# A four-layer transformer kernel on one core: the row normalization of both attention stages divided over two head pairs, one step to a block of units

## The reference, cut to what matters

```python
def reference(...):
    x = L0_attn_x                                   # (4, 1024, 128)
    x = _layernorm(x + _L0_attn_ref(x, ...))        # 16 heads of 64, causal        (stage s0)
    x = _layernorm(x + _L0_ffn_ref(x, ...))         # gated attention, 8 heads      (stage s1)
    x = _layernorm(x + _L1_attn_ref(x, ...))        # 16 heads of 64, relative bias (stage s2)
    x = _layernorm(x + _L1_ffn_ref(x, ...))         # 16 experts, top 32 tokens
    return x

def _layernorm(x, axis=-1, eps=1e-05):
    m = jnp.mean(x, axis=axis, keepdims=True)
    v = jnp.var(x, axis=axis, keepdims=True)
    return (x - m) / jnp.sqrt(v + eps)
```

## Time and profile before

| | |
|---|---|
| median of 3 runs | 4331.12 us (4328.69 to 4333.49) |
| the profiled execution | 4329.32 us, span of its trace 4327.6 us |
| PE busy | 3832.9 us, 89% of the span |
| DVE busy | 3238.8 us, 75% |
| POOL busy | 2941.0 us, 68% |
| ACT busy | 1926.0 us, 45% |
| mean granted clock of PE | 0.954 of full |
| stage s0 | about 50 to 1150 us |
| stage s2 | about 2550 to 4190 us |

### The profile page before, as it was taken

One profiled execution on the slowest core, in us unless ns is written; L12 is line 12 of the kernel. 1 busy time (PEld: TensorE's weight loads), 2 busy tenths in 40 slices (PEclk: granted clock), 3 DMA queues, 4 the chain that ended last, 5 costly groups with the idle time before them and its releaser, 6 DMA issues. The chain is left out here.

```text
span 4327.6 us, 62571 instructions
## 1 busy us (share of the span) xinstructions
PE 3832.9 (89%) x22170; PEld 2166.8 (50%) x22170; DVE 3238.8 (75%) x5670; ACT 1926.0 (45%) x3478; POOL 2941.0 (68%) x2166
## 2 busy tenths in 40 slices
PE   7998998989788989889899848999999999999964
PEld 4554555545355555555555424555455445545533
DVE  5887868868487877877877647887888788878826
ACT  3443544434354555454455313444444344434423
POOL 2776767757445877877887926777777677767740
PEclk9999999999888999999999958999999999999987
DMA  3000000000110000100100031211222121212121
GB/s 55 23 20 15 24 14 25 10 6 1 40 46 19 28 28 19 38 28 19 33 28 10 6 63 28 43 30 30 40 38 37 30 40 30 45 26 39 19 59 30
DMA packets 98072, 125.87 MB, mean 29 GB/s; under 512 B 28929, under 2 KB 76481, under 8 KB 97761
## 3 DMA queue, kind: packets, MB, share of 16 engines
q1 hardware_dynamic: 97760, 121.86, 13.1%
HBM read 103.69 MB, written 18.12 MB: 28 GB/s over the span
## 5 line engine op out<-in xcount | busy, mean ns | idle before, releaser
L857 POOL TENSOR_TENSOR s_psum_p<-s_psum_p,s_prob 128x1024 f32<-128x1024 f32 (+3 forms) x640 | 1335.5, 2087 | 371.0 <-ACT s_prob L562 320.7
L562 ACT ACTIVATE s_prob<-s_sT 128x1024 f32<-128x1024 f32 (+2 forms) x896 | 791.8, 931 | 843.4 <-DVE s_sT L713 473.8
L459 PE MATMUL s_pv<-s_prob,s_vp 128*64 128x512 f32 (+3 forms) x3584 | 795.7, 565 | 4.8 <-POOL s_prob L842 4.8
L669 DVE CUSTOM_DVE_ANT_0 s_mx<-s_mx,s_strip 128x512 f32<-128x512 f32 x628 | 421.8, 713 | 162.4 <-PE s_mx L415 159.1
L1746 POOL TENSOR_TENSOR s_psum_p<-s_psum_p,s_prob 128x1024 f32<-128x1024 f32 x192 | 462.5, 2409 | 105.9 <-ACT s_prob L1469 104.1
L1469 ACT ACTIVATE s_prob<-s_sT 128x1024 f32<-128x1024 f32 x256 | 262.7, 1026 | 585.5 <-PE s_sT L1333 585.5
L415 PE MATMUL s_mx<-s_bh,s_ah 64*128 64x512 f32 (+2 forms) x1756 | 396.2, 447 | 102.9 <-DVE s_bm L659 58.7
L718 DVE RECIPROCAL s_recip<-s_recip 128x128 f32<-128x128 f32 x512 | 452.5, 921 | 35.5 <-ACT s_recip L509 35.5
L857 POOL TENSOR_TENSOR s_psum_p<-s_prob 128x1024 f32<-128x1024 f32 (+1 forms) x128 | 288.5, 2254 | 197.0 <-ACT s_prob L562 194.3
L459 PEld LDWEIGHTS s_pv<-s_prob,s_vp 128*64 128x64 f32 x3584 | 218.8, 137 | 371.7 <-issue 288.3
L415 PEld LDWEIGHTS s_mx<-s_bh,s_ah 64*128 64x128 f32 x1756 | 165.8, 185 | 449.9 <-issue 191.0
(11 more groups left out here) (291 smaller groups left out, 7256.3 us busy)
## 6 DMA issues: line engine op xcount, KB each, us to landing
s_strip<-bias_rows SPq DMA_DIRECT2D x256, 144.0 KB, 5.7
s_wr<-gated_weights SPq DMA_DIRECT2D x32, 960.0 KB, 4.8
s_near<-bias_rows SPq DMA_DIRECT2D x256, 48.0 KB, 2.0
x<-s_x SPq DMA_DIRECT2D x10, 512.0 KB, 3.4
s_x<-x SPq DMA_DIRECT2D x8, 512.0 KB, 5.1
gated_weights<-s_side_hi SPq DMA_DIRECT2D x8, 480.0 KB, 2.6
gated_weights<-s_side_lo SPq DMA_DIRECT2D x8, 480.0 KB, 2.9
s_x<-in_L_attn_x_dram SPq DMA_DIRECT2D x4, 512.0 KB, 5.3
```

Source lines behind the costliest of these rows:

```text
L459: last = mm(pv[heads(hd), lo:CH], vp[:, g // VP % 2, j, at:at + DH], prob[:, k % PR, hd, lo:CH], start=j == 0, stop=end)
L562: nc.scalar.activation(prob[:, k % PR, :, lo:CH], sT[:, k % 2, :, lo:CH], ACT.Exp, scale=st.scale).then_inc(exp_done, 1)
L669: last = nc.vector.tensor_tensor_reduce(out=mx[:, hd, :], in0=mx[:, hd, :], in1=strip[:, g % 2, hd, first:first + CH], scale=1.0, scalar=N ...
L857: nc.gpsimd.tensor_tensor(out[:, :, lo:CH], src, p[:, :, lo:CH], ALU.add)\
```

## The change

In `Pairs.jobs` the seven steps no longer all stand in pair 1 of the next batch. Steps 0 to 3 stay there, steps 4 to 6 go to pair 2, and each gets a block to itself.

```diff
@@ -165,9 +165,12 @@
         if g > 0:
             out[3].append(("norm", 2 * g - 2))
             out[7 if self.causal or after else 9].append(("norm", 2 * g - 1))
-        if p == 1 and b > 0:
-            for n, u in enumerate((3, 4, 5, 6, 7, 8, 10) if self.causal else (5, 6, 7, 8, 9, 10, 12)):
-                out[u].append(("ln", b - 1, n))
+        if b > 0:
+            first = (3, 5, 7, 9) if self.causal else (5, 7, 9, 13)
+            rest = (3, 5, 9) if self.causal else (5, 7, 11)
+            for n, (of, u) in enumerate([(1, u) for u in first] + [(2, u) for u in rest]):
+                if p == of:
+                    out[u].append(("ln", b - 1, n))
         return out
```

## The result

| | before | after |
|---|---|---|
| median | 4330.07 us (6 runs) | 4380.04 us (4373.02 to 4384.75, 6 runs) |
| ratio to before, 95% interval | | 1.0117 [1.0103, 1.0131] |
| span of the profiled execution | 4327.6 us | 4380.0 us |
| mean granted clock | 0.954 | 0.95 |

What follows compares the result with a forecast made beforehand. PE was taken to set the pace, with DVE close behind and tied to it. Stall 47.5 plus clock 7.5 minus spreading gains 10 and 4 made +41 us on 4329.3, forecast 4372 us, range 4345 to 4392.

Steps and rivals of the forecast that it cites:

- the likeliest case: Whole kernel: stalls of 44 to 52 us in s2 with the smaller clock loss, 4372 us, chance 0.66.
- Part 3, the stall: s2, block 12 of pair 2: DVE's first maximum waits for strips queued behind the late store, 47.5 us lost.
- Part 3's place: s2, first maximum of block 12 in pair 2: the strip wait is on the path, each microsecond also lost by PE.
- The first rival: Block 12 of pair 2: no strip wait, only the gains remain, -14 us, 4317 us, chance 0.07.
- The second: Block 12 of pair 2: PE's other work rides out 6 us of each stall, clock stays up, 4347 us, chance 0.12.
- The third: Behind each stall: PE stays at half clock for 14 us, losing 7 us a time, 4386 us, chance 0.15.
- Part 4, the clock: Behind each of three stalls in s2: some 5 us of PE work at half rate, 7.5 us lost in all.
- a loss of half of that: Behind each stall: half of some 5 us of half-rate PE work is lost, 2.5 us, three times.
- Part 1, spreading in s2: s2: giving each step its own block wins 3.4 us a batch, 10 us in all, bounds 0 and 19.8.
- Step 5 is an 8-column instruction: nothing: s2, pair 2: the sixth of the seven steps, counted from 0, costs no time in its new block.
- Part 2, spreading in s0: s0: at most one step in each block of a pair gives a small gain of 4 us, bounds 0 and 18.
- I take 1.3 us a batch of the 6.0: s0: of the 6.0 us the seven steps cost per batch, spreading wins 1.3 us, 4 us in all.

Runs made afterwards that it cites:

- the repeat: The changed kernel itself, unaltered, run again beside a kernel with filler products on PE: 4384.92 us, ratio 1.0127.
- the narrow additions: Changed kernel with SP's store behind the strips, and POOL's additions cut to 16 of 512 columns in pair 2 of s2: 4324.54 us, ratio 0.9982.
- s0 alone: The changed kernel with the new places of the seven steps only in s0, s2 keeping the old ones: 4338.44 us, ratio 1.0011.

## Why the prediction was right, and which terms were not

The verdict, the range and the mechanism that decides held: the likeliest case came, and 4380 is 8 us above the forecast. Two of the four terms had the wrong sign all the same, so the small distance is in part luck. By its own parts:

- **Part 3, the stall: right.** Waits of 15.4, 15.4 and 11.9 us were in the sum (3.45 + 0.42 + 11.5, and 0.4 + 11.5); the profile has 15.80, 15.88 and 12.82. On the path it is 42.3 us, with what the lower clock behind the stalls costs in it: pairs 2 and 3 take 340.6 us together in the change and 298.3 with the store behind the strips. I had 47.5, since I added 1.6 us each for step 6 in front of it, and in the run with the store behind that cost is there without any stall.
- **Part 3's place: right.** Wherever step 6 stood directly ahead of that maximum and the store ahead of the strips, the stall was there. SP waited 39.5, 36.3 and 37.9 us, where some 30 had been given. The first rival (no stall, 4317) has nothing for it. The second (6 us of each stall ridden out) neither: PE stood 18.2, 18.0 and 15.0 us. The third (the clock costs more, 4386) comes near in its time, above all to the 4384.92 us of the repeat, but not by its reason: the lower clock behind a stall lasted 3.5 to 3.8 us and not 14.
- **Part 4, the clock: right in kind, wrong in size.** The lower clock came behind each stall, for 3.5 to 3.8 us and not 5, but DVE covers it: at most about 2 us against 7.5. The step that failed is "a loss of half of that". It took PE for the engine that sets the pace in block 12, while part 3 had just said that PE waits for DVE there. By the rule of the Trainium skill (TensorE: Matmul & The Clock Gate, Terms), throttled time times one minus the ratio, these 11 us of work at the lower clock would cost an estimated 5.5 us. The measurement differs and decides here: PE's own work does get longer, but not the kernel by as much.
- **Part 1, spreading in s2: wrong sign.** Forecast 10 us won. With the stall away, pair 1 wins 2.5 us a batch (the 3.24 us of PE behind steps 1 and 2 shrank to 1.95, as forecast), but pairs 2 and 3 lose 17.7 us in all (298.3 against 280.6): together some 10 us lost. The steps that failed are "Step 5 is an 8-column instruction: nothing" (1.93 us, and PE stood 1.95) and the length of step 6, 1.90 us taken, 2.86 measured. Both are waits for POOL's additions, as the narrow additions showed. The odd 1.97 us of step 1 was in the rows, and the prediction itself names a wait for POOL as its reason; I weighed it only for a chance to win. It should have been asked of each step: does it meet POOL at work?
- **Part 2, spreading in s0: wrong sign.** Forecast 4 us won, measured 3.6 us lost in the profile of the change and 5.7 between the medians with s0 alone. Steps 2 and 3 alone took 2.20 and 1.95 us there where 1.23 and 1.16 had been, again across POOL's work, while step 6 won 0.4 to 1.1 us. The step that failed is "I take 1.3 us a batch of the 6.0": it took the lengths of the steps as fixed. A longer s0 was among the signs of being wrong, and it came. That these waits are the whole loss of s0 is argued and not shown: no run took POOL's additions away in s0. One reading is that two steps in one block wait for POOL once, and two steps in two blocks can wait twice.
- **The sum.** Forecast 47.5 + 7.5 - 10 - 4 = 41. The runs give 42 for stall and clock together, 10 for the spreading in s2 and 4 to 6 for s0, 56 to 58 us; the medians say 50, and 54.5 in the repeat. The parts were measured in separate runs, each uncertain by a few microseconds, so they do not close to better than that. Stall and clock had been taken 13 us too high, the two terms of spreading 28 to 30 us too low. These errors cancel out in part, and only in part: the total is a better forecast than its terms.

## What to carry to other kernels

Before moving a step, list who waits for its semaphore and what stands in that queue behind the wait. Here a store that nobody was waiting for held up the strip that DVE's very next instruction needed, and the price was the whole latency of store, load and strip pieces, some 15 us each time. Put what is needed soon ahead of what waits for something late; it cost nothing in the kernel before (4332.72 against 4332.76 us) and leaves 5.7 us of the change's loss.

Spreading work evenly over blocks is a gain only if each piece fits beside what the other engines do at that moment. Read a small instruction with a long duration as a wait, and find what ends with it.

## What the runs showed of the hardware that was not expected

- A DVE instruction on 8 columns takes 0.11 us when POOL's additions are short and 1.93 us when it begins during a 128x1024 addition, and ends within 0.05 us of that addition. A 128x1024 multiply of two SBUF operands takes 1.16 to 2.86 us by the same cause. Reductions of one operand are not touched (1.16 to 1.22 us).
- POOL pays as well. In the run with the store behind the strips, its two additions took 5.70 us where step 3 ran beside them, and 4.9 us elsewhere; POOL's timeline, then DVE's:

```profile
3886.47 5.70 POOL L860 TENSOR_TENSOR s_psum_p<-s_psum_p,s_prob 128x1024 f32<-128x1024 f32 x2 [1.96 <-ACT s_prob L565]
```

```profile
3888.43 1.47 DVE L765 TENSOR_TENSOR s_yT<-s_x 128x1024 f32<-128x1024 f32 x1
```

- Half of the granted clock for 3.5 to 3.8 us right behind a stall cost the kernel at most about 2 us in three times, and 3.4 us of it in a pair of s2 cost 0.2 to 1.0 us. The same 1.95 us of idle PE was followed by the lower clock in some batches and not in others.
